# Turning copies in halves, and TensorE's tile loop written out with one expert read per tile

## The reference, cut to what matters

```python
x = x + tanh(g_xattn) * xattn(layernorm(x), fside, ctx)     # int8-style products, the first part
# the second part, the mixture of experts; T = 1024 tokens, H 256, I 896, E 8, K 2, R 64
conf = sigmoid(xn @ conf_W.T + conf_b); bids = conf * wealth
top_bids, sel = top_k(bids, 2); routing = softmax(top_bids)
for e in range(8):
    g = xn @ base_gate + xn @ gate_A[e] @ gate_B[e] / 4
    u = xn @ base_up   + xn @ up_A[e]   @ up_B[e]   / 4
    h = silu(g) * u
    oe = h @ base_down + h @ down_A[e] @ down_B[e] / 4
    out += weight_of(e) * oe
x = x + tanh(g_ffn) * out
```

## Time and profile before

| | us |
|---|---|
| median of 3 runs | 287.29 (286.26 to 287.44) |
| the profiled execution | 284.62 |
| its span | 282.5 |
| PE busy in the span | 245.4 (87%) |
| DVE, ACT, POOL busy | 193.6, 175.2, 131.5 |

### The profile page before, as it was taken

The page is one execution under the profiler, slowest core; times in us unless marked ns, Lnnn a source line. Parts: engine busy times, 40 slices in busy tenths (PEclk is TensorE's granted clock), DMA queues, the critical chain, the costliest instruction groups (busy, mean ns, idle before and its releaser), DMA issues.

```text
span 282.5 us, 5150 instructions
## 1 busy us (share of the span) xinstructions
PE 245.4 (87%) x1550; PEld 220.0 (78%) x1551; DVE 193.6 (69%) x407; ACT 175.2 (62%) x378; POOL 131.5 (47%) x152
## 2 busy tenths in 40 slices
PE   0857567899989999998856999999999999999893
PEld 0746455689979988898756998888888888888792
DVE  2979978778379824367654678766677676666754
ACT  3336898998656357569765476566666655566450
POOL 4488575585830111365521674885344444321151
PEclk9977797799999999999995999999999999999979
DMA  5943532465994495363440244545444445440554
GB/s 164 338 125 84 140 100 69 131 202 194 285 310 166 177 329 212 93 203 152 148 148 22 78 150 167 169 158 178 167 167 167 157 158 167 166 148 21 145 173 148
DMA packets 31345, 45.73 MB, mean 162 GB/s; under 512 B 14104, under 2 KB 25760, under 8 KB 31328
## 3 DMA queue, kind: packets, MB, share of 16 engines
q0 software_dynamic: 4416, 21.50, 22.6%
q1 hardware_dynamic: 20752, 14.03, 18.3%
q10 hardware_dynamic: 6160, 9.98, 9.9%
HBM read 33.57 MB, written 11.93 MB: 161 GB/s over the span
## 4 chain that ended last, share of the span: by engine, by line
PE 62%; DVE 16%; ACT 7%; DMA 5%; issue 5%; POOL 2%; ACTq 1%; SPq 0%; DVEq 0%
PE pY L56 8%; PE pY L60 7%; PE pY L58 7%; PE pT L1766 4%; PE bank L56 3%; PE bank L58 3%; PE bank L60 3%; PE pX L56 3%; PE pG L1755 2%; DMA x_resid<-in_x_dram 2%; PE pG L1756 2%; PE pU L1755 2%; PE pU L1756 2%; DVE bank L1057 2%; DVE q L1054 2%
## 5 line engine op out<-in xcount | busy, mean ns | idle before, releaser
L56 PE MATMUL pY<-Wd_hi,hT_hi 128*128 128x320 f32 (+1 forms) x126 | 42.1, 334 | 0.1
L60 PE MATMUL pY<-Wd_hi,hT_lo 128*128 128x320 f32 (+1 forms) x126 | 39.7, 315 | 0.0
L58 PE MATMUL pY<-Wd_lo,hT_hi 128*128 128x320 f32 (+1 forms) x126 | 39.7, 315 | 0.0
L559 POOL DMA_INDIRECT xin<-normed,tok x19 | 18.5, 975 | 43.4 <-PE pX L1716 26.9
L567 POOL DMA_INDIRECT bin<-base_products,tok x18 | 20.3, 1128 | 31.8 <-DVE hbuf L1351 23.0
L573 POOL DMA_INDIRECT results<-yb,dest x17 | 16.9, 994 | 29.3 <-ACT yb L903 28.4
L1361 DVE TENSOR_TENSOR hT_lo<-pT,hT_hi 128x512 fp32r<-128x512 f32 (+1 forms) x38 | 23.5, 620 | 4.5 <-ACT hT_hi L880 3.5
L56 PE MATMUL bank<-Wbase_hi,x2T_hi 128*128 128x448 f32 x64 | 24.6, 384 | 0.8 <-ACT brow L735 0.8
L735 ACT COPY brow<-bank 128x448 f32<-128x448 f32 x32 | 16.9, 532 | 13.3 <-PE bank L60 12.7
L56 PEld LDWEIGHTS pY<-Wd_hi,hT_hi 128*128 128x128 f32 x126 | 23.7, 188 | 0.5 <-ACT Wd_lo L869 0.5
L58 PEld LDWEIGHTS pY<-Wd_lo,hT_hi 128*128 128x128 f32 x126 | 23.8, 189 | 0.0
(11 more groups left out here) (330 smaller groups left out, 723.0 us busy)
## 6 DMA issues: line engine op xcount, KB each, us to landing
base_products<-brow ACTq DMA_DIRECT2D x16, 448.0 KB, 3.5
yr<-results SPq DMA_DIRECT2D x8, 256.0 KB, 5.0
raw<-in_L_ffn_gate_B_dram SPq DMA_DIRECT2D x8, 224.0 KB, 2.6
raw<-in_L_ffn_up_B_dram SPq DMA_DIRECT2D x8, 224.0 KB, 3.1
raw<-in_L_ffn_down_A_dram SPq DMA_DIRECT2D x7, 256.0 KB, 4.6
x_resid<-in_x_dram SPq DMA_DIRECT2D x4, 256.0 KB, 5.2
q<-in_fside_BxS2xS_dram ACTq DMA_DIRECT2D x4, 256.0 KB, 6.7
normed<-q ACTq DMA_DIRECT2D x4, 256.0 KB, 3.9
```

Of the source, the lines that this page charges most:

```text
L56: m.matmul(outs[i], hi, whi[i], start=first, stop=False, skip_group_check=True)
L58: m.matmul(outs[i], hi, wlo[i], start=False, stop=False, skip_group_check=True)
L60: ins = m.matmul(outs[i], lo, whi[i], start=False, stop=last, skip_group_check=True)
L559: g.indirect_dma_start(out=xin[:, :], out_offset=None, in_=xn, in_offset=bass.IndirectOffsetOnAxis(ap=tok[:, j:j + 1], axis=0)).then_inc(d ...
```

## The change

The turning copies for B are split into a gate half and an up half (64 x 896 each) on ACT and DVE, so `s_crossed` and `s_turned` count to 8 for B and to 9 with the one for down_B. They move into the tiles: ACT's go mostly between `silu`, `xa_hi` and `z_out`, DVE's around `h_mul`. POOL holds each pair one place earlier in its queue. TensorE's loop becomes straight code, and every expert's number is read once, two tiles ahead, between the down products of chunks 4 and 5.

```diff
 # POOL
             pool.wait_ge(s_direct, 1)
             gather_base(1)
             pool.wait_ge(s_direct, 2)
+            hold_B(0)                 # hold_B(g) waits s_turned >= 2 * (g - 1) for g >= 2
             gather_base(2)
-            hold_B(0)
+            hold_B(1)
             for j in range(3, PT + 4 - LATE):
                 if j < PT:
                     gather(j)
-                if j - 2 < G:
-                    hold_B(j - 2)
+                if j - 1 < G:
+                    hold_B(j - 1)
                 if j >= 4:
                     scatter(j - 4)
                 if j < PT:
                     gather_base(j)
 # ACT, tile(j); G = 4
                 down_A_expert(j - 1, 0, e)
                 z_hi(j - 2)
+                j == 2: cross_B(1, 0)         j == 3: cross_B(2, 1)
                 x_hi(j + 1); h_hi(j - 1, 0); down_A_expert(j - 1, 1, e); y_out(j - 2)
                 h_hi(j - 1, 1); xa_out(j + 1); silu(j)
+                j == 3: cross_B(3, 0)
                 xa_hi(j + 1)
+                j == 1: cross_B(0, 0), cross_B(0, 1)
+                j == 2: cross_B(1, 1), cross_B(2, 0)
+                j == 3: cross_B(3, 1)         j == 5: cross_dB()
                 z_out(j - 1)
-            cross_B(0) after tile 1, cross_B(1) after 2, cross_B(2), cross_B(3) after 3, cross_dB after 5
 # DVE, tile(j)
                 z_lo(j - 2)
+                j == 3: turn_B(2, 1)
                 x_lo(j + 1); h_lo(j - 1, 0); g_add(j); h_lo(j - 1, 1); u_add(j); xa_lo(j + 1)
+                j == 3: turn_B(3, 0)
                 h_mul(j)
+                j == 1: turn_B(0, 0), turn_B(0, 1)
+                j == 2: turn_B(1, 0), turn_B(1, 1), turn_B(2, 0)
+                j == 3: turn_B(3, 1)          j == 5: turn_dB()
 # TensorE
-                        pe.wait_ge(s_turned, G)
+                        pe.wait_ge(s_turned, 2 * G - 1 + gu)    # before expand_B(4, gu)
             def tile(j, back2=True, last=False):
-                e = expert(j)
+                e = experts[j]
...
-                    down_B_products(j - 2, expert(j - 2))
+                    down_B_products(j - 2, experts[j - 2])
...
-                    project_A(j + 1, expert(j + 1))
+                    project_A(j + 1, experts[j + 1])
                 down_products(j - 1, range(0, 3), not back2)
                 xa_T(j + 1)
-                down_products(j - 1, range(3, IC), not back2)
+                down_products(j - 1, range(3, 5), not back2)
+                if j >= 2:
+                    next_expert()          # value_load of expert j + 2
+                down_products(j - 1, range(5, IC), not back2)
...
-            for j in range(2, G + 4):
+            for j in range(2, PT - 1):
                 tile(j)
-            with pe.Fori(G + 4, PT - 2, 2) as j:
-                tile(j)
-                tile(j + 1)
```

More of the change, by code:

```diff
@@ L583, in _, with hold_B @@
                 pool.wait_ge(d_bn[i], 16 * len(range(i, 2 * NT, 3)))
+            def hold_B(g):
+                if g >= 2:
+                    pool.wait_ge(s_turned, 2 * (g - 1))
+                nc.gpsimd.tensor_copy(held_B[:, g % 2], pair_B(g, 0)).then_inc(s_held, 1)
             pool.wait_ge(s_direct, 1)
@@ L624, in _ @@
                 if j == 8:
-                    pool.wait_ge(s_turned, G + 1)
+                    pool.wait_ge(s_turned, 2 * G + 1)
                 if 8 <= j < 8 + LATE:
@@ L911, in tile @@
                     z_hi(j - 2, not back3)
+                if isinstance(j, int) and j == G - 2:
+                    cross_B(1, 0)
+                if isinstance(j, int) and j == G - 1:
+                    cross_B(2, 1)
                 if not last:
@@ L921, in tile, with cross_B, cross_dB @@
                 silu(j)
+                if isinstance(j, int) and j == G - 1:
+                    cross_B(3, 0)
                 if not last:
                     xa_hi(j + 1)
+                if isinstance(j, int) and j == G - 3:
+                    cross_B(0, 0)
+                    cross_B(0, 1)
+                if isinstance(j, int) and j == G - 2:
+                    cross_B(1, 1)
+                    cross_B(2, 0)
+                if isinstance(j, int) and j == G - 1:
+                    cross_B(3, 1)
+                if isinstance(j, int) and j == G + 1:
+                    cross_dB()
                 z_out(j - 1, not back2)
-            def cross_B(g):
+            def cross_B(g, gu):
                 act.wait_ge(s_held, g + 1)
-                act.wait_ge(s_g, g + 1)
-                act.wait_ge(s_u, g + 1)
-                a.copy(pair_B(g, 0)[R:P], pair_B(g, 1)[0:R]).then_inc(s_crossed, 1)
+                act.wait_ge((s_g, s_u)[gu], g + 1)
+                a.copy(pair_B(g, 0)[R:P, gu], pair_B(g, 1)[0:R, gu]).then_inc(s_crossed, 1)
+            def cross_dB():
+                act.wait_ge(s_held, G + 1)
+                act.wait_ge(s_y, G)
+                a.copy(pair_dB(0)[R:P], pair_dB(1)[0:R]).then_inc(s_crossed, 1)
             x_hi(0)
@@ L951, in _ @@
             tile(1, back2=False)
-            cross_B(0)
             for j in range(2, G + 2):
                 tile(j, back3=(j > 2))
[L955 to L961, removed]
             with act.Fori(G + 2, PT - 1) as j:
@@ L1371, in tile @@
                     z_lo(j - 2)
+                if isinstance(j, int) and j == G - 1:
+                    turn_B(2, 1)
                 if not last:
@@ L1379, in tile @@
                     xa_lo(j + 1)
+                if isinstance(j, int) and j == G - 1:
+                    turn_B(3, 0)
                 h_mul(j)
+                if isinstance(j, int) and j == G - 3:
+                    turn_B(0, 0)
+                    turn_B(0, 1)
+                if isinstance(j, int) and j == G - 2:
+                    turn_B(1, 0)
+                    turn_B(1, 1)
+                    turn_B(2, 0)
+                if isinstance(j, int) and j == G - 1:
+                    turn_B(3, 1)
+                if isinstance(j, int) and j == G + 1:
+                    turn_dB()
             def late_lo(n):
@@ L1388, in _, with turn_B, turn_dB @@
             dve.wait_ge(s_resid, NB)
-            def turn_B(g):
-                dve.wait_ge(s_crossed, g + 1)
-                v.tensor_copy(pair_B(g, 1)[0:R], held_B[R:P, g % 2]).then_inc(s_turned, 1)
+            def turn_B(g, gu):
+                dve.wait_ge(s_crossed, 2 * g + gu + 1)
+                v.tensor_copy(pair_B(g, 1)[0:R, gu], held_B[R:P, g % 2, gu]).then_inc(s_turned, 1)
+            def turn_dB():
+                dve.wait_ge(s_crossed, 2 * G + 1)
+                v.tensor_copy(pair_dB(1)[0:R], held_dB[R:P]).then_inc(s_turned, 1)
             x_lo(0)
@@ L1703, in _, with next_expert @@
             ins.then_inc(s_latep, 1)
[L1705 to L1709, removed]
+            experts = [GE * j for j in range(G)]
+            def next_expert():
+                j = len(experts)
+                if j < PT:
+                    experts.append(pe.value_load(eid[0:1, j:j + 1], min_val=0, max_val=E - 1))
             def x_T(j):
@@ L1854, in _ @@
             pe.wait_ge(s_wlo, CH_A)
-            project_A(0, expert(0))
+            project_A(0, experts[0])
             unit(28)
@@ L1861, in _ @@
             unit(4 * NT - 1)
-            project_A(1, expert(1))
+            project_A(1, experts[1])
             for gu in range(2):
                 for i in range(2):
-                    expand_B(0, gu, i, expert(0), True)
+                    expand_B(0, gu, i, experts[0], True)
             xa_T(1)
@@ L1879, in _ @@
             h_T(PT - 1, 1)
-            down_B_products(PT - 2, expert(PT - 2))
-            last_down_A(expert(PT - 1))
+            down_B_products(PT - 2, experts[PT - 2])
+            last_down_A(experts[PT - 1])
             last_down(range(0, 4))
@@ L1884, in _ @@
             last_down(range(4, IC))
-            down_B_products(PT - 1, expert(PT - 1), pG[:, 0, 0:H])
+            down_B_products(PT - 1, experts[PT - 1], pG[:, 0, 0:H])
             pe.wait_ge(s_onehot, LATE)
```

12 lines of the change are left out of this document (1 added, 11 removed).

## The result

The change makes the kernel faster: 275.56 us in the median of 4 runs (274.08 to 278.73) beside 286.77 us of the kernel before in the same sitting (285.14 to 287.44). The ratio is 0.960 with an interval of 0.952 to 0.968. The forecast was 274.3 with a range of 271.5 to 279. The profiled execution took 274.08 us with a span of 272.0; before it was 284.62 and 282.5. So 10.5 us of the span are to be found.

A forecast was written before the change was run, and what follows sets the result against it. TensorE bounds the last phase from about 100 us on, other engines only where it waits. Terms 7.8 + 0.3 + 0.3 + 4.6 = 13.0 us, off the 287.29 us median, give 274.3; own range 272.5 to 276.5, whole range 271.5 to 279.

The forecast's parts named there:

- The large stall and its clock: Ahead of tile 4: PE's 5.2 us wait for DVE's copy and 2.6 us of low clock go, together 7.8 us.
- The clock's price: Tile 4 up to its first down product takes 6.57 us at clock 0.50, 3.93 in tile 5; 2.6 us go.
- Tiles 2 and 3: Two waits of 0.85 us for z_lo go (1.7), a new stall of 1.4 us comes: 0.3 us gained.
- The new wait: Tile 3's down products wait about 1.4 us for y_out(1), because scatter(0) is issued behind hold_B(3).
- The port: DVE and POOL share it; DVE's half turn, started first, is stretched by hold_B(3); otherwise POOL loses 0.5 us.
- The reads: Tiles 6 to 17: one read per expert amid queued down products saves 12 x 0.38 = 4.6 us.
- the down_B turn: Moved ahead of z_out(4) into ACT's idle time; PE's 0.3 us wait in tile 6 goes.
- hole: 0.38 us between last B product pair and first down product, 1.40 us in tile 12 against 1.02 in tile 5.
- Rival B: The 0.38 us a tile comes from register addresses or queue refill, not the read, and stays: 278.9 us; chance 0.13.
- D: Slower: TensorE's straight code must be fetched and its sequencer runs dry, 294 us at 2 us a tile; chance 0.05.
- C: No new stall in tile 3: scatter lands within 2 us or POOL reaches it sooner, 272.9 us; chance 0.15.
- A: Tile 3's new stall grows to 3.3 us and brings the clock down as the old one did: 278.8 us; chance 0.12.

The follow-up runs named there:

- e6: The kernel before with 24 products whose result nobody reads, ahead of PE's wait for DVE's last turn in tile 4: 283.76 us, ratio 0.991.
- e5: The change with scatter(j-4) ahead of hold_B(j-1) in POOL's loop: 274.13 us, ratio 0.9555 to the kernel before.
- e9: e5 with ACT's z_hi(j-2) ahead of the first copy of down_A: 273.46 us, ratio 0.958 to the kernel before.
- e10: e9 with POOL's late_rows() behind gather(7) instead of ahead of it: 272.46 us, ratio 0.953 to the kernel before.
- e2: The kernel before with only TensorE's new straight loop and reads, turning copies as before: 281.30 us, ratio 0.984.
- e7: The change with scatter(0) and gather_base(4) both ahead of hold_B(3) on POOL: 274.25 us, ratio 0.957 to the kernel before.
- e3: The change with TensorE's straight loop, but the expert's number read at each of three uses as before: 278.53 us, ratio 0.973 to the kernel before.
- e4: The change with its one read per tile moved directly ahead of project_A, behind the wait for z_lo: 279.21 us, ratio 0.976 to the kernel before.
- e1: The change's turning copies and POOL order, with TensorE's loop and reads as in the kernel before: 278.57 us, ratio 0.976 to that kernel.
- e8: The change itself, unaltered, run again in another sitting: 274.82 us (271.94 to 278.10), ratio 0.955 to the kernel before.

## Why the prediction was right, and where it was not

The time came out inside the forecast's own range (275.56 us, forecast 274.3), and the saving is 11.2 us where 13.0 were predicted. The two mechanisms that carry the sum, the stall with its clock and the reads, are there. One term was 1 us too large, and one size was met partly by luck.

**The large stall and its clock: 7.8 predicted.** The 5.2 us are gone, and turns 7 and 8 come in time but for some 0.3 us ahead of turn 7. The clock's price was right: e6 shows 2.9 us where the prediction took 2.6. But tile 4 doesn't run at the ideal 3.93 us. It takes 4.77, because `x_T(5)` waits 0.76 us for `gather(5)`. This is the step that failed: "(139.7, landed at 143.3 by the median of the earlier trace rows), used by `g_add(4)` and `x_T(5)` in tile 4, after 145: nothing". The gather was issued at 142.43. Of these 2.7 us, 1.66 had been lost before `x_T(3)` (the later start and `gather(3)`); with them added the hold began just as forecast (135.8 + 1.66 = 137.46). The other 1.1 are the hold's longer run and the longer issues and gaps behind it. And the gather landed 6.1 us after its issue, later than any of the earlier trace rows (5.3 at most); either of the two alone would have left no wait. From tile 3's first down product to tile 4's first product the gain is 5.05 us (9.33 and 4.28), in tile 4's stretch 1.80 (6.57 and 4.77): the term was worth 6.85 us.

**Tiles 2 and 3: 1.7 - 1.4 = 0.3 predicted.** Both waits for `z_lo` are gone; tile 2 gave 0.71 us. The new wait is 1.43 us and stands where it was put, with the cause that was named: e5 takes the hold from ahead of the scatter, and the wait disappears. That its size was met is partly luck. With the same 1.66 us added, the scatter was issued 0.5 us later than forecast; the copy behind it started 2.75 us after the issue, less than the 2.9 that were taken from another line's scatters as the least; and PE came 0.3 us late to its wait. The tiles' own scatters (L573) in the kernel after:

```profile
DMA to landing us min/median/max: 2.4/2.5/5.2
```

`gather(3)` was issued behind the two holds as forecast (124.17; forecast 122.6, and 1.5 for the later start) and cost 0.16 us, which was taken as nothing. Tile 3 lost 0.91 us up to its down products: 142.86 - 136.28 = 6.58, where it was 5.67 (from 135.50 on, the same product before). The wait gone is +0.85, the new one -1.43, and some 0.3 us were lost ahead of `project_A(4)` (140.55), which the prediction doesn't have. So the term is -0.2 us.

**The port: half wrong.** The prediction went by a row, a DVE multiplication stretched by a copy of POOL that started behind it. In the kernel after the engine that started first kept its time, whichever it was. DVE's three half turns are whole:

```profile
136.24 1.70 DVE L1421 CAST WB<-held_B 64x896 fp32r<-64x896 f32 x3
...
138.13 0.29 DVE L1380 TENSOR_TENSOR zT_lo<-pY,zT_hi 128x128 fp32r<-128x128 f32 x1 [0.20 <-ACT zT_hi L898]
...
139.10 0.86 DVE L1421 CAST WB<-held_B 64x896 fp32r<-64x896 f32 x1 [0.67 <-ACT WB L947]
```

and POOL's hold, which started during the third of them, took 2.02 us instead of 1.68. It is the Trainium skill's rule (SBUF — State Buffer, two separate sides: the first to start has the pair of ports for its whole instruction) that this trace agrees with here, at a price of 0.34 us; the prediction had 0.5 for the case that the rule holds. The next half turn, (2,1), started at 139.10 inside the hold and took 0.86 us, where the one at 148.04 took 0.62; in e9 and e10, where it starts behind the hold's end, it takes 0.66 and 0.67. Behind it stands `x_lo(4)`, which ends at 140.41, and then `project_A(4)` at 140.55: these are the 0.3 us of the paragraph above. They cost nothing here, since PE waited until 142.86 anyway. `z_lo(1)` was not late. The row at 159.86 is no single case. The same multiplication took 2.37 us in e2 and 2.61 in e5 and e7, where POOL's copy starts 0.36 and 0.6 us behind it; where the copy starts 0.8 us behind, as in the kernel after (155.50 and 154.69), the multiplication takes 1.08 us and the copy 1.17. So the order of the starts in the rows doesn't always tell who loses. Why is open; POOL issues a gather right before that copy in all of these traces.

**The reads: 4.6 predicted.** Measured: 0.377 us on average in the ten intervals from `x_T(8)` on, 0.26 at 7->8 (e2, which has only the new reads, has 7.49 there; the other 0.39 is the down_B turn's, predicted as 0.3), and 0.35 in tile 17 of the tail's 1.00, 4.4 us in all. The size was right and the reason half of it: e3 and e4 show that 0.25 us are the read behind the wait for `z_lo` and that 0.10 to 0.13 belong to the loop. The argument that tile 5 has no hole as "the first is missing, since expert 3's tile is mixed, and the sequencer stays ahead" doesn't hold: e4 leaves the first read out everywhere and keeps the hole from tile 6 on. What differs in tile 5 is that z's low part ends 0.31 to 0.34 us before PE comes to it, in the traces of the kernel before, e3 and e4, and only 0.14 or 0.15 us before in every tile from 6 to 17, where PE has waited for it. That the wait empties PE's queue, and the read stays hidden where there is none, fits all of these rows and was not tested by itself. Rival B had a true part, 0.10 to 0.13 us of the 0.38, which the straight loop removes all the same; so the sum didn't notice it. That the looped tiles and not tiles 6 and 7 have it could be read before the change: 1.29 and 1.31 us there, 1.38 to 1.42 in the loop.

**Other rivals.** D, fetching of straight code, shows nowhere: PE is busy 88.00 of 88.00 us, and e3's straight tiles are shorter than e1's looped ones with the same reads. C came about in neither profiled execution of the change. A is no rare event: of the five profiled executions that have this stall (the change, e1, e3, e4, e8) it came in mildly in one (e1) and fully in one (e8, 278.10 us, where A said 278.8). The median escaped it. The runs of the change reach from 271.94 to 278.73 us, some 2.5%, where those of the kernel before reach from 283.69 to 287.79 over all sittings, 1.4%. I read that as the scatter's landing, which e8 shows in one execution; for the runs without a profile it is not shown, and e3 and e4, which have the same scatter in the same place, lie within 1.0 us in four runs each.

**The sum.** 6.85 for the stall and the clock (7.8), -0.2 for tiles 2 and 3 (0.3), 0.4 for tile 6 (0.3) and 4.4 for the reads (4.6) make 11.45 us where 13.0 were predicted. 0.6 us more come from the tail, whose clock before was 0.79 from 265 to 273 us and after stays at 1.00 until 270.9; that this is the reason is read from the two traces and not tested. The late start of the phase takes 1.5. That makes 10.55 us, and the spans differ by 10.5. In medians the gain was 11.2 and 10.8 us (e8), by the ratios 11.5 and 12.9: all near the sum without the last two, and too far apart to tell it from 13.0.

## What to carry to other kernels

Before moving an operation in a DMA-issuing engine's queue, go through everything behind it until the first issue whose buffer is waited for: here a 1.7 us copy, put ahead of a scatter, cost 1.4 us through a single buffer and 0.8 through a gather that had looked free. Give such landings at least the longest value of the trace and not the median, since all later tiles pay for one late landing; here even the longest (5.3 us) was passed (6.1). Register reads cost 0.25 us right behind a wait, one or three alike, and a read amid queued products cost nothing: look for its place before its number.

## What the hardware showed that was not expected

A stall of 1.42 us (e1) was followed by a granted clock of 0.50 from 143.2 to 146.4 us, stalls of 1.43 and 1.44 us (the change, e3, e4) by 1.00 throughout, and one of 3.4 us (e8) by 0.50; the length of the stall alone doesn't settle it. Indirect transfers landed late without a change in their issue: the same scatter let its waiter go 2.75 to 2.77 us after its issue in four traces (the change, e1, e3, e4) and 4.7 us in one (e8), and gathers went up to 6.1 us (5.3 at most before). Filling a stall with products that nobody needs made the kernel before 2.7 us faster in the median. And DVE and POOL stretched each other's copies in turn (2.02 us for 1.68, then 0.86 for 0.62) when each started inside the other's.
